# Layer 3 attention of a four-layer network on one Trainium2 core: eleven of twelve chunks of the powers split, low parts of values on VectorE, both casts on ScalarE, one-input operations for the maxima's parts

## The reference

```python
def _L3_xattn_ref(q_input, kv_input, key_padding_mask, W_Q, b_Q, W_K, b_K, W_V, b_V, W_O, b_O):
    q = q_input @ W_Q + b_Q
    k = kv_input @ W_K + b_K
    v = kv_input @ W_V + b_V
    q = q.reshape(B, LQ, N_HEAD, D_H).transpose(0, 2, 1, 3)   # k and v alike
    ...
    sim = jnp.einsum('bhqd,bhkd->bhqk', q, k) / jnp.sqrt(jnp.float32(D_H))
    sim = jnp.where(mask, neg_inf, sim)
    attn = jax.nn.softmax(sim, axis=-1)
    out = jnp.einsum('bhqk,bhkd->bhqd', attn, v)
    return out.transpose(0, 2, 1, 3).reshape(B, LQ, D_MODEL) @ W_O + b_O

x = x + _L3_xattn_ref(_layernorm(x, axis=-1), ctx_1024, mask_BxS2_bk0, ...)
```

## Time and profile before

| | |
|---|---|
| median of 3 runs | 1952.28 us (1950.78 to 1955.94) |
| profiled execution, its own time | 1950.98 us |
| its span | 1949.2 us, mean granted clock 0.916 |
| PE busy | 1635.3 us (84%) |
| VectorE (DVE) busy | 1369.9 us (70%) |
| ScalarE (ACT) busy | 930.4 us (48%) |
| GpSimd (POOL) busy | 700.4 us (36%) |

### The profile page before, as it was taken

How to read it: one execution, slowest core, us unless ns; L and a number is a source line. 1 busy time by engine, 2 the same in 40 slices (tenths; PEclk the granted TensorE clock), 3 DMA queues, 4 the chain that set the end, 5 groups by cost and what they waited for, 6 DMA issues and landing times. The chain is left out here.

```text
span 1949.2 us, 30882 instructions
## 1 busy us (share of the span) xinstructions
PE 1635.3 (84%) x10566; PEld 1381.4 (71%) x10566; DVE 1369.9 (70%) x2269; ACT 930.4 (48%) x1342; POOL 700.4 (36%) x607
## 2 busy tenths in 40 slices
PE   3994686427899999999999975799999999996896
PEld 2994475216799999999999942477777777774795
DVE  5215543674788888888888823588888888884598
ACT  1332221203566666666666502466666666662332
POOL 0110000000323332333233100487778877773231
PEclk8897798656899999999999997899999999998798
DMA  2015492004211111111111001353535253430110
GB/s 53 23 43 128 116 247 46 1 0 109 64 33 33 33 61 32 32 32 61 33 32 32 0 3 25 88 113 83 112 76 119 66 121 73 114 66 3 55 44 20
DMA packets 98144, 118.10 MB, mean 61 GB/s; under 512 B 16833, under 2 KB 82914, under 8 KB 98082
## 3 DMA queue, kind: packets, MB, share of 16 engines
q1 hardware_dynamic: 98082, 117.32, 24.2%
HBM read 78.51 MB, written 0.46 MB: 41 GB/s over the span
## 5 line engine op out<-in xcount | busy, mean ns | idle before, releaser
L2211 POOL TENSOR_TENSOR l3att_PL<-l3att_P,l3att_PH 125x1120 fp32r<-125x1120 f32 x128 | 330.2, 2579 | 121.1 <-DVE l3att_PH L2292 61.3
L1608 ACT CAST l2att_PT<-PS 125x512 fp32r<-125x512 f32 x336 | 175.5, 594 | 221.5 <-PE PS L1543 221.5
L1673 DVE TENSOR_REDUCE l2att_neg<-PS 128x1 f32<-128x1500 f32 x112 | 192.7, 1721 | 75.3 <-PE PS L1536 75.2
L2113 ACT ACTIVATE l3att_P<-PS 125x1344 f32<-125x1344 f32 x128 | 165.5, 1293 | 136.3 <-PE PS L1993 134.3
L1679 DVE TENSOR_TENSOR l2att_PT<-PS,l2att_PT 125x512 fp32r<-125x512 f32 x336 | 210.4, 681 | 2.0 <-ACT l2att_PT L1608 2.0
L1499 POOL CAST l_QH<-l_QP 128x128 fp32r (+1 forms) x112 | 54.1, 483 | 381.0 <-POOLq L1288 219.5
L1543 PEld LDWEIGHTS PS<-all_ident,l2att_P 128*125 128x125 f32 x1344 | 164.8, 189 | 14.6 <-DVE l2att_P L1687 6.0
L1617 ACT ACTIVATE l2att_P<-PS,l2att_neg 128x1500 f32<-128x1500 f32 x112 | 171.2, 1528 | 5.2 <-DVE l2att_neg L1673 5.2
L1575 PE MATMUL PS<-l2att_PT,l2att_cc 125*128 125x256 f32 x576 | 170.7, 296 | 0.0
L1543 PE MATMUL PS<-all_ident,l2att_P 128*125 128x128 f32 x1344 | 166.6, 274 | 4.6 <-DVE l2att_P L1687 4.6
L1577 PE MATMUL PS<-l2att_PT,l2att_cc 125*128 125x256 f32 x576 | 162.9, 283 | 0.0
(11 more groups left out here) (510 smaller groups left out, 3765.3 us busy)
## 6 DMA issues: line engine op xcount, KB each, us to landing
l3att_KS<-l3att_kh SPq DMA_DIRECT2D x128, 187.5 KB, 4.0
l_cT<-in_ctxT SPq DMA_DIRECT2D x8, 1500.0 KB, 11.2
l_cT<-in_ctxT SPq DMA_DIRECT2D x16, 750.0 KB
l_c<-in_ctx SPq DMA_DIRECT2D x16, 750.0 KB
l3att_cT<-in_ctxT SPq DMA_DIRECT2D x16, 750.0 KB, 4.8
l3att_KS<-l3att_kl SPq DMA_DIRECT2D x64, 187.5 KB, 3.8
l_c<-in_ctx SPq DMA_DIRECT2D x8, 1344.0 KB
l0f_w<-in_L_ffn_W SPq DMA_DIRECT2D x16, 256.0 KB, 3.1
```

Of the source, the lines that this page charges most:

```text
L1608: act.copy(PT[:, 4 * g:4 * g + 4, PLACE[u1], 0, :], PS[0:CHUNK, 3 * s1 + g, :].rearrange("k (c r) -> k c r", r=128)).then_inc(hi_in, 1)
L1673: v.tensor_reduce(neg[:, s:s + 1], E, XY_AXES, ALU.max, negate=True).then_inc(top_in, 1)
L2113: act.activation(P[s][:, PART * part:PART * part + PART, :].rearrange("p (i j) r -> p i (j r)", j=2), PS[0:CHUNK, 3:6, 0:2 * SET_ROWS], AC ...
L2211: g.tensor_tensor(PL[s][:, part, :, :], P[s][:, PART * part:PART * part + SPLIT, :], PH[s][:, part, :, :], ALU.subtract).then_inc(pl_in, 1)
```

## The change

- Chunk 5 is split as well: `HALVED` = 11, PH and PL hold 11 chunks, of which 6 belong to the first half and 5 to the second; only chunk 11 is plain.
- Both casts to PH are on ScalarE, each behind its Exp.
- The low part of the values is computed by VectorE from PSUM and the high part, between the query copy and the first reduction; ScalarE's copy VF and GpSimd's subtraction go, and PE's T0 waits for the low part where it waited for VF.
- The two parts of the negated maxima are made by a `tensor_reduce` over one element and by two `tensor_scalar` of one element per partition, where a `tensor_copy` and a `tensor_tensor` were.
- WOS moves into the space of XN; it is cleared by GpSimd after the first query blocks, and SP's loads of it wait for that (`wos_clear`).
- VectorE waits for its earlier multiplication (`on_in`) before the reciprocal.

```diff
-SPLIT = PART - 1
+HALVED = CHUNKS - 1
...
-            WOS = self.sb(whole, "WOS", [SETS * VCOLS, SETS, D])
+            WOS = self.XN[0:SETS * VCOLS, 0:SETS, :]
...
                     if b == 0:
-                        sp.wait_ge(cleared, 1)
+                        sp.wait_ge(wos_clear, 1)
...
-                                pe.wait_ge(vf_in, thirds)
+                                pe.wait_ge(vl_in, thirds)
...
-                            if k % PART < SPLIT:
+                            if k < HALVED:
...
                 act.copy(heads(s, i)[:, :, 0:8], src).then_inc(vh_in, 1)
-                act.wait_ge(vl_in, b * BANKS + i)
-                act.copy(VF[:, :, :], src).then_inc(vf_in, 1)
...
-                    def high_part():
-                        act.wait_ge(p_in, 2 * n - 1)
-                        act.copy(PH[s][:, 0, :, :], P[s][:, 0:SPLIT, :]).then_inc(ph_in, 1)
+                    def high_part(part):
+                        some = slice(PART * part, min(PART * part + PART, HALVED))
+                        act.wait_ge(p_in, 2 * n - 1 + part)
+                        act.copy(PH[s][:, some, :], P[s][:, some, :]).then_inc(ph_in, 1)
...
                         powers(0)
-                        high_part()
+                        high_part(0)
                         powers(1)
+                        high_part(1)
...
-                chain(g.memset(WOS[:, :, :], 0.0))
...
-                def low_values(b, s, i):
-                    g.wait_ge(vf_in, b * BANKS + i + 1)
-                    g.tensor_tensor(heads(s, i)[:, :, 8:16], VF[:, :, :], heads(s, i)[:, :, 0:8], ALU.subtract
-                                    ).then_inc(vl_in, 1)
...
+                g.wait_ge(xt_ps, 2)
+                g.memset(WOS, 0.0).then_inc(wos_clear, 1)
...
-                            g.tensor_tensor(PL[s][:, part, :, :], P[s][:, PART * part:PART * part + SPLIT, :],
-                                            PH[s][:, part, :, :], ALU.subtract).then_inc(pl_in, 1)
+                            some = slice(PART * part, min(PART * part + PART, HALVED))
+                            g.tensor_tensor(PL[s][:, some, :], P[s][:, some, :], PH[s][:, some, :],
+                                            ALU.subtract).then_inc(pl_in, 1)
...
+                def low_values(b, s, i, bank):
+                    v.wait_ge(vh_in, b * BANKS + i + 1)
+                    v.tensor_tensor(heads(s, i)[:, :, 8:16], PS[0:CHUNK, bank, :].rearrange("p (x j) -> p x j", j=8),
+                                    heads(s, i)[:, :, 0:8], ALU.subtract).then_inc(vl_in, 1)
...
                 for n in range(2 * SETS):
                     scaled(n)
+                    if n < BANKS:
+                        low_values(0, 0, n, 3 + n)
                 v.wait_ge(cleared, 1)
+                v.sem_inc(on_in, 1)
...
                         v.wait_ge(den_ps, (n - SETS) // SETS)
+                        v.wait_ge(on_in, (n - SETS) // SETS)
...
+                    if g == 3 and live(known, 1, GROUPS - SETS):
+                        low_values(b + 1, 1 - u // SETS, 0, 5)
+                    if g == 0 and live(known, 1, GROUPS - SETS):
+                        low_values(b, u // SETS, 1, 5)
+                    if g == 1 and (known is None or SETS < known < GROUPS):
+                        low_values(b, u // SETS, 2, 5)
...
-                        v.tensor_copy(negs[:, u % 2, :, 1], negm[:, u % 2, :]).then_inc(nh_in, 1)
+                        v.tensor_reduce(negs[:, u % 2, :, 1], negm[:, u % 2, :].unsqueeze(2), X_AXIS, ALU.max
+                                        ).then_inc(nh_in, 1)
                         v.wait_ge(nh_in, n + 1)
-                        v.tensor_tensor(negs[:, u % 2, :, 2], negm[:, u % 2, :], negs[:, u % 2, :, 1],
-                                        ALU.subtract).then_inc(negs_in, 1)
-                    if live(known, 1, GROUPS):
-                        s = (u - 1) % 2
-                        v.wait_ge(p_in, 2 * n)
-                        if known is None or known >= 3:
-                            v.wait_ge(o_ps, n - 2)
-                        v.tensor_copy(PH[s][:, 1, :, :], P[s][:, PART:PART + SPLIT, :]).then_inc(ph_in, 1)
+                        for half in range(2):
+                            last = v.tensor_scalar(negs[:, u % 2, half, 2:3], negm[:, u % 2, half:half + 1],
+                                                   negs[:, u % 2, half, 1:2].bitcast(F32), None, ALU.subtract)
+                        last.then_inc(negs_in, 1)
```

More of the change, by code:

```diff
@@ L1801, in attend_sets @@
             cT = [self.sb(ctx, f"cT{s}", [128, KEYS]) for s in range(2)]
-            VF = self.sb(ctx, "VF", [CHUNK, 64, 8])
             SEL = self.sb(ctx, "SEL", [ROWS17, SETS, VCOLS])
@@ L1825, in attend_sets @@
             P = [self.sb(ctx, f"P{s}", [CHUNK, CHUNKS, SET_ROWS]) for s in range(2)]
-            PH, PL = ([self.sb(ctx, f"{n}{s}", [CHUNK, 2, SPLIT, SET_ROWS], F32R) for s in range(2)]
+            PH, PL = ([self.sb(ctx, f"{n}{s}", [CHUNK, HALVED, SET_ROWS], F32R) for s in range(2)]
                       for n in ("PH", "PL"))
@@ L1833, in attend_sets @@
                  "maskb_in"))
-            (k_ps, kh_in, kl_in, v_ps, vh_in, vf_in, vl_in, den_ps, inv_in, on_in, qb_in, sr_ps, top_in, nh_in, negs_in, t_ps, m_in,
+            (k_ps, kh_in, kl_in, v_ps, vh_in, vl_in, wos_clear, den_ps, inv_in, on_in, qb_in, sr_ps, top_in, nh_in, negs_in, t_ps, m_in,
              st_ps, p_in, ph_in, pl_in, o_ps, o_in) = (self.sem(ctx, n) for n in (
-                 "k_ps", "kh_in", "kl_in", "v_ps", "vh_in", "vf_in", "vl_in", "den_ps", "inv_in", "on_in", "qb_in", "sr_ps", "top_in", "nh_in",
+                 "k_ps", "kh_in", "kl_in", "v_ps", "vh_in", "vl_in", "wos_clear", "den_ps", "inv_in", "on_in", "qb_in", "sr_ps", "top_in", "nh_in",
                  "negs_in", "t_ps", "m_in", "st_ps", "p_in", "ph_in", "pl_in", "o_ps", "o_in"))
@@ L2020, in values @@
                             first, last = k == 0, k == CHUNKS - 2
-                            if k % PART < SPLIT:
-                                pe.matmul(out, VS[s][:, k, g, :], PH[u % 2][:, k // PART, k % PART, :],
+                            if k < HALVED:
+                                pe.matmul(out, VS[s][:, k, g, :], PH[u % 2][:, k, :],
                                           start=first, stop=False)
-                                mm = pe.matmul(out, VS[s][:, k, g, :], PL[u % 2][:, k // PART, k % PART, :],
+                                mm = pe.matmul(out, VS[s][:, k, g, :], PL[u % 2][:, k, :],
                                                start=False, stop=last)
@@ L2184, in block_queries @@
                         BM[:, :].unsqueeze(2).to_broadcast([96, SETS, TOK]), ALU.mult).then_inc(qb_in, 1)
-                for i in range(BANKS):
-                    low_values(0, 0, i)
-                g.wait_ge(vl_in, BANKS)
                 for n in range(2 * SETS):
@@ L2193, in _ @@
                     block_queries(0, 0, x)
+                g.wait_ge(xt_ps, 2)
+                g.memset(WOS, 0.0).then_inc(wos_clear, 1)
                 def one(n, u, known):
                     b, x = n // SETS, u % SETS
-                    if x == 3 and live(known, 1, GROUPS - SETS):
-                        low_values(b + 1, 1 - u // SETS, 0)
-                    if x == 0 and live(known, 1, GROUPS - SETS):
-                        low_values(b, u // SETS, 1)
-                    if x == 1 and (known is None or SETS < known < GROUPS):
-                        low_values(b, u // SETS, 2)
                     if known is None or known < GROUPS - SETS:
@@ L2282, in one @@
                             v.wait_ge(t_ps, n - 1)
-                        v.tensor_copy(negs[:, u % 2, :, 1], negm[:, u % 2, :]).then_inc(nh_in, 1)
+                        v.tensor_reduce(negs[:, u % 2, :, 1], negm[:, u % 2, :].unsqueeze(2), X_AXIS, ALU.max
+                                        ).then_inc(nh_in, 1)
                         v.wait_ge(nh_in, n + 1)
-                        v.tensor_tensor(negs[:, u % 2, :, 2], negm[:, u % 2, :], negs[:, u % 2, :, 1],
-                                        ALU.subtract).then_inc(negs_in, 1)
-                    if live(known, 1, GROUPS):
-                        s = (u - 1) % 2
-                        v.wait_ge(p_in, 2 * n)
-                        if known is None or known >= 3:
-                            v.wait_ge(o_ps, n - 2)
-                        v.tensor_copy(PH[s][:, 1, :, :], P[s][:, PART:PART + SPLIT, :]).then_inc(ph_in, 1)
+                        for half in range(2):
+                            last = v.tensor_scalar(negs[:, u % 2, half, 2:3], negm[:, u % 2, half:half + 1],
+                                                   negs[:, u % 2, half, 1:2].bitcast(F32), None, ALU.subtract)
+                        last.then_inc(negs_in, 1)
                 run_steps(v, GROUPS, LAG, UNROLL, one, peeled=1)
-                v.wait_ge(on_in, BATCH)
```

(1 more changed line is left out.)

## The result

The changed kernel takes 1987.12 us (median of 4 runs, 1981.1 to 1990.56), the kernel before, on the same chip, 1952.74: ratio 1.0162, 95% interval 1.0146 to 1.0178. It is slower, by 34 us; the prediction had 1977 and 1950 to 1990. The profiled execution took 1984.65 us, its span 1982.9 us, mean granted clock 0.913.

What follows compares the result with a forecast made beforehand. The prediction took the ring through GpSimd's first subtraction and V1 as the bound: +1.75 us a batch over 15.5 batches is 27.1, less 1.7 setup, +25.4 on 1950.98; with 1.3 for the median, 1977 us, range 1950 to 1990.

Steps and rivals of the forecast that it cites:

- The ring: Per step, query copy through Exp, cast, first subtraction and V1 to next copy: 7.94 us becoming 8.62, 8.75 with low values.
- A: Faster: V1 not held by the longer subtraction, low values hold up nothing; 17.4 us off, 1935; chance 0.12.
- B: No change: subtraction covered, low values pay 0.4 us in three steps of four; 1954 us; chance 0.08.
- The low values: VectorE makes them before the first reduction, T0's fifth matmul waits: +0.13 us in three steps of four.
- The reliefs: Query copy no longer held by the reciprocal, 0.90 us a batch, nor by VectorE's L2223, 0.11.
- The maxima: VectorE's L2283 waits for GpSimd, but V1's wait covers it: removal costed at nothing, instead of 70 us.
- rival C: Much slower: new one-element subtractions on VectorE wait for GpSimd, maxima 1.8 us later a step; 112 more, 2089; chance 0.06.
- Setup: GpSimd's three low-value subtractions no longer stand ahead of the eight L2177: -1.7 us, between 0 and -3.75.
- The clock: Granted clock kept at 1.00, although PE gets idle times of about 1 us.
- the tail: Last group: second subtraction no longer behind VectorE's 0.74 us cast, paying for 0.68 of longer parts: nothing.
- The sum: 62 steady steps, 15.5 batches x 1.75 = 27.1 us, less 1.7 in the setup: +25.4 us.

Runs made afterwards that it cites:

- e1: The changed kernel with chunk 5 multiplied as plain fp32 again, so both halves' casts and subtractions have five chunks; 1952.3 us.
- e6: The changed kernel with GpSimd's first subtraction in two instructions, chunks 0 to 3 and 4 to 5, V1 waiting for the first alone; 1950.6 us.
- e2: The changed kernel with the low parts of the values back on GpSimd, from ScalarE's plain copy; 1974.6 us.
- e4: The kernel before with only the maxima's parts made by the new operations; 1947.7 us.
- e5: The changed kernel with the old cast and two-input subtraction for the maxima's parts; 2076.2 us.
- e14: The changed kernel with PE's maxima and R0 ahead of V1, ScalarE's second cast later, first subtraction in two pieces, low values on GpSimd; 1930.4 us.

## Why the prediction was right, and where it was off

**The ring** was right, piece by piece. From the cast to the subtraction it is 1.39 for 1.20 (+0.19 as forecast; the cast itself takes 1.31 for 1.13), from the subtraction to V1 3.17 where 2.56 + 0.49 + 0.13 = 3.18 was forecast, and a step without low values 8.55 for 8.62. e1 takes the longer pieces away and the loss goes; e6 keeps them and only relieves V1, and it goes as well. Both speak against rivals A and B, which had the subtraction covered. (These two priced the relief at the low keys once a batch; by the forecast's own figures the batch before held 33.12 - 4 x 7.94 = 1.36 above its ring and not 1.01, so A stood for about 23 us and not 17.4. And 1976.4 + 1.3 is 1977.7, not 1977.)

**The low values** were mis-sized by more than a factor of two. The term was +0.13, measured +0.29 (e2). It had VectorE begin them 0.30 after the query copy's start, as L2223 follows L2292 with an overlap of 0.08; here L2215 follows at 0.42, behind the whole 0.38 of the copy. It takes 0.04 less than the 0.73 assumed, so it ends at 1.11 for 1.03, and the fifth matmul's weights load at 1.16 for 1.06. That is 0.10 of the 0.16 missed; the other 0.06 pass between those weights and Exp (0.52, where the forecast's terms leave 1.39 - 0.93 = 0.46). The 0.16 counts in three steps of four, and the ring without low values came 0.07 below its 8.62, so that the batch grew by 1.95 and not by 1.75: 3 x 8.84 + 8.55 = 35.07.

**The reliefs** came as forecast: no query copy waits for the reciprocal, and the 0.11 at the low keys is gone. Counted from the forecast's own terms, 4 x 0.68 + 3 x 0.29 - 0.90 - 0.44 = 2.25 would be more than the 1.95 seen; the difference is about the 0.07 by which each step's ring came out below 8.62, most of it the shorter way from V1 to the query copy (1.28 for 1.33).

**The maxima** were right to within 4 us: the wait was all but covered, and its removal alone is worth that much (e4). The Trainium skill ("SBUF — State Buffer", Who interferes with whom) is right about who waits (1.3 us with a cast, 0.16 with `tensor_reduce`), but a wait only counts on the path. What the prediction missed is that the edit was needed: it considered the two subtractions' collision for the new operations (rival C) and not for the old ones beside the cast on ScalarE, where e5 shows it at 89 us, some of them through the clock.

**Rival C** is refuted: the two `tensor_scalar` take 0.34 us together beside GpSimd's work, in e4 and in the changed kernel. The rule of the Trainium skill ("VectorE: DVE Perf Modes", What auto-detection actually checks), which leaves open what one element a partition does, does not hold them up here.

**Setup** gave 1.0 for the 1.7 forecast, for the reason named there: GpSimd's first L2177 (now L2170) starts 1.0 earlier in the stage, and VectorE's three subtractions stand between the scalings.

**The clock and the tail** are the step that failed. The prediction kept 1.00 to the end and priced the tail at nothing, from PE's idle times of about 1 us in the steady steps; but in the last steps PE is idle for 1.7 to 2.3 us at a time, the granted clock fell, and the end took 5.1 us more. The last three intervals are 8.94, 9.45 and 10.06 us at a mean clock of 1.00, 0.90 and 0.84, where before they were 8.00, 7.98 and 8.87 at 1.00. The first of them shows the ring alone. The ring without low values and with the 0.1 of the last steps would give 8.65 in the other two, which leaves 0.8 and 1.4 that come with the clock, and perhaps some of the 1.5 behind the last copy: an estimate of 2 to 4 us. The longer ring is not shown to be what brings the clock down. e4, whose steady steps are no longer than before, lost it at the same place:

```profile
1752.59:1761.35 8.76, 6.94 (x45) 5.72 (x44) 5.71 (x8) 3.94 (x4) 5.92 (x3) 0.89 0.02 5
```

There PE had been idle before V1 for 1.66 and 1.68 us, and in the kernel before for 1.68 and 1.67, where the clock stayed at 1.00. So what decides it stays open. No run tried the clock alone.

**The sum.** The forecast was +25.4 (27.1 less 1.7), measured were +33.7 in the span, 8.3 more. The intervals between query copies gave 2.4 + 28.2 + 3.6 = 34.2 for the 27.1, that is 7.1 more; about 3 of it is the 0.2 by which a steady batch was forecast too short, the rest lies in the first batch, in the last steps and in the clock. Behind the last query copy it is 1.5 more, in the setup 0.7 more, in the layers before 1.5 less, and in the rest 0.5 more. The 1.5 of the layers before, which the change does not touch, is luck in the forecast's favour.

## What to carry to other kernels

Find the ring by adding start to start until it closes, and check it with an edit that keeps the work but releases the waiting engine sooner, as e6 does: it costs a few lines and tells length from wait. An edit on one engine gains only up to the next bound: here PE's order alone gave 17 us, the piecewise subtraction alone 36, each with ScalarE's order 40, and all three 45. Price an edit together with its neighbours, since the same two lines were worth 4 us alone and 89 beside the others; and look at first and last steps separately, where work that fills the gaps is missing.

## What the runs showed of the hardware that was not expected

- A `tensor_tensor` of two elements a partition on VectorE took 2.48 us (e5), the whole of GpSimd's second subtraction. It starts at 1416.84, just after the first subtraction's end (1416.78) and 0.10 behind the start recorded for the second (1416.74). L2275, which had stood waiting since before such a boundary, went first there. By these rows the first of such a pair gets its turn at the boundary, and the second comes too late for it. In e5 it alternates: at 1407.72, with both starting within 0.01 us, the pair took 1.30 and 0.16.
- When both sides collide, both can lengthen. In e14 the multiplication by the reciprocal took 0.89 us for 0.38: it started at 1408.29 beside a subtraction of GpSimd that ended at 1408.93, and ended 0.25 after it. GpSimd's next instruction, the low values, took 1.41 for 1.25 beside it:

```profile
1408.29 0.89 DVE L2280 TENSOR_TENSOR l_OC<-l_OC,l3att_inv 68x224 f32 x1
...
1408.89 1.41 POOL L2173 TENSOR_TENSOR l3att_VS<-all_XN,l3att_VS 125x512 fp32r<-125x512 f32 x1
```

- GpSimd's subtraction is linear in its length: 2.09 us for 896 elements (e14), 2.57 for 1120, 3.05 for 1344, about 2.15 ns an element and 0.17 us beside.
